# Drains and woven statistics in the GAT passes of a graph network, and a weight product moved between its two GCN passes

## What is computed

```python
h = relu(layernorm(x));  x = x + gat(elu(gat(h, W1)), W2)   # two GAT layers, 4 heads, self loops
h = relu(layernorm(x));  x = x + attention(h)               # 8 heads, exp(clip(q.k)), sum / (z + 1e-9)
h = relu(layernorm(x));  x = x + hyperbolic(h)
h = relu(layernorm(x))
def gcn(x, W, b): return relu(segment_sum((x @ W)[src] * norm, dst) + b)
x = x + (gcn(gcn(h, W6, b6), W7, b7) @ Wp + bp)
```

## Time and profile before

| | us |
|---|---|
| three runs | 6064.08, 6054.41, 6054.90 |
| median | 6054.9 |
| the profiled execution | 6061.28 |
| its span | 6059.5 |
| mean granted TensorE clock, share of full | 0.903 |

### The profile page before, as it was taken

The page is one execution under the profiler, slowest core; times in us unless marked ns, Lnnn a source line. Parts: engine busy times, 40 slices in busy tenths (PEclk is TensorE's granted clock), DMA queues, the critical chain, the costliest instruction groups (busy, mean ns, idle before and its releaser), DMA issues. The chain is left out here.

```text
span 6059.5 us, 76838 instructions
## 1 busy us (share of the span) xinstructions
PE 4625.8 (76%) x20970; PEld 3391.5 (56%) x20970; DVE 4623.4 (76%) x13469; ACT 3032.3 (50%) x7622; POOL 3524.5 (58%) x3009
## 2 busy tenths in 40 slices
PE   4888888888884888856777688888857658996665
PEld 3666666666662666634665455555534435664554
DVE  5888888888886888838999467777768878884555
ACT  2777777777771444423444345555535544441111
POOL 3555454444525777728888277777634425446777
PEclk9999999999996999977888889999977879998877
DMA  3666666666663444425777534544437764444444
GB/s 119 236 243 240 244 241 245 238 242 243 242 232 116 126 127 127 128 72 192 252 240 250 174 117 152 153 154 154 147 111 242 248 220 129 147 138 126 144 152 137
DMA packets 651890, 1096.80 MB, mean 181 GB/s; under 512 B 88662, under 2 KB 472086, under 8 KB 651341
## 3 DMA queue, kind: packets, MB, share of 16 engines
q1 hardware_dynamic: 526026, 837.10, 40.4%
q0 software_dynamic: 125440, 254.79, 14.3%
HBM read 523.88 MB, written 575.95 MB: 182 GB/s over the span
## 5 line engine op out<-in xcount | busy, mean ns | idle before, releaser
L839 PE MATMUL mm<-w,tt 128*128 128x264 f32 x3136 | 737.3, 389 | 0.8 <-ACT tt L883 0.8
L1321 POOL DMA_INDIRECT aim<-F,index x392 | 592.9, 1512 | 119.5 <-issue 119.5
L839 PEld LDWEIGHTS mm<-w,tt 128*128 128x128 f32 x3136 | 585.7, 192 | 92.6 <-ACT tt L883 1.0
L777 POOL DMA_INDIRECT xd<-in_x_dram,index x196 | 219.5, 1120 | 681.3 <-DMA XD<-xd 650.4
L1321 POOL DMA_INDIRECT got<-F,index x392 | 495.5, 1264 | 167.7 <-issue 108.5
L1477 ACT ACTIVATE rows<-acc 128x260 f32<-128x260 f32 (+1 forms) x588 | 227.3, 387 | 646.4 <-PE acc L1468 646.3
L805 POOL DMA_INDIRECT place<-PLACE,place_ix x392 | 425.4, 1085 | 119.5 <-issue 119.5
L1464 PE MATMUL acc<-got,sel 128*128 128x260 f32 (+1 forms) x1176 | 432.7, 455 | 78.9 <-DVE sel L1440 72.5
L829 PE MATMUL tp<-ident,h 128*128 128x128 f32 x1568 | 236.8, 284 | 325.2 <-ACT h L894 163.3
L2476 DVE SCALAR_TENSOR_TENSOR agg<-mask,agg,acc 128x128 f32<-128x128 f32 x784 | 237.5, 345 | 248.5 <-issue 143.8
L839 PE MATMUL mm<-wl,tt 128*128 128x264 f32 x1568 | 421.7, 391 | 5.7 <-ACT tt L883 5.4
(11 more groups left out here) (349 smaller groups left out, 13762.5 us busy)
## 6 DMA issues: line engine op xcount, KB each, us to landing
F<-f1o SPq DMA_DIRECT2D x97, 528.0 KB
F<-f2o SPq DMA_DIRECT2D x97, 528.0 KB, 3.3
HL<-ho SPq DMA_DIRECT2D x97, 528.0 KB, 3.7
xin<-in_x_dram SPq DMA_DIRECT2D x97, 512.0 KB
H<-h SPq DMA_DIRECT2D x97, 512.0 KB, 3.6
X<-x3o SPq DMA_DIRECT2D x97, 512.0 KB, 2.6
out_dram<-oo SPq DMA_DIRECT2D x97, 512.0 KB
drow<-DSTF SPq DMA_DIRECT2D x84, 448.0 KB
```

What stands on the lines that cost most here:

```text
L777: nc.gpsimd.indirect_dma_start(out=xd[:, n % 2, t, :], out_offset=None, in_=x, in_offset=bass.IndirectOffsetOnAxis(ap=index[:, tile, 1:2], ...
L839: last = nc.tensor.matmul(mm[PAIR[stage, q]][:, r, 0:F2W], lhs[:, q, 2 * r + k, :], w[:, k, :], start=(k == 0), stop=(k == KB - 1))
L1321: nc.gpsimd.indirect_dma_start(out=buf[:, n % SLOTS, t, :], out_offset=None, in_=table, in_offset=bass.IndirectOffsetOnAxis(ap=index[:, n ...
```

## The change

1. SoftPass gets `make_way(dve)`: it issues two steps of a generator that the stage may have set (`self.steps`), then a drain of DVE if the stage has `yields` set. GAT1 and GAT2 set it, the hyperbolic pass does not. It stands after the backward scan, after each piece of the message, after `sel`, after the pieces of the own part in `gat_output` (GAT2), and after the first piece of its sum and of its quotient; in GAT1 also after each piece of the ELU and of the own part. That is 10 drains a group in GAT1 and 8 in GAT2.
2. In GAT2 the statistics of group n - 3 (before: n - 2) are issued two steps at each `make_way`, with the rest after the differences. What follows them moves one group: the stores of H2 (n - 4) and Q2 (n - 6), ACT's normalization (n - 4), the product with Wq (n - 5). The loops of DVE, PE, ACT and SP get one iteration more.
3. In the attention pass POOL issues the four degree gathers before `got[1]`.
4. In the first GCN pass the product with W7 is gone. PE multiplies `agg` by W6 into rows of edges, with b6 added by a matmul of ones with three bf16 parts (`b6_parts`); ACT takes the relu to `put`, so T7 holds relu(agg W6 + b6). The statistics are woven into `carry_on`, two steps after each of its eight operations; `carry_on` works for group n - 3 (before n - 2), `select` for n - 1 (before n).
5. In the second GCN pass PE multiplies `agg` by W7 (four matmuls of 128x512 a group) and ACT takes relu and b7 from that.
6. Setup: the constant rows of T7 are relu(b6) with no product; `b6_parts` is made; the load of b6 as a column is gone.

The core of the diff:

```diff
+            def make_way(self, dve):
+
+                take(self.steps, 2)
+                if self.yields:
+                    dve.drain()
...
                 V.tensor_tensor_scan(self.bwd[:, s, ::-1], self.pen[:, s, 1:SE + 1][:, ::-1], self.fwd[:, ::-1], -BIG,
                                      ALU.add, ALU.max).then_inc(self.done["most"], 1)
+                self.make_way(dve)
...
                     V.tensor_tensor(by_head(g[:, k, 0:D], H), by_head(g[:, k, 0:D], H),
                                     per_head(self.w_edge(n)[:, k, :], D // H), ALU.mult)
+                    self.make_way(dve)
...
-                        last = V.tensor_tensor(by_head(o[:, k, :], H), by_head(own[:, k, :], H),
-                                               per_head(self.w_own(n)[:, k, :], D // H), ALU.mult)
-                    link(last)
+                        last = link.go(V.tensor_tensor(by_head(o[:, k, :], H), by_head(own[:, k, :], H),
+                                                       per_head(self.w_own(n)[:, k, :], D // H), ALU.mult))
+                        self.make_way(dve)
+                    link.need(last)
                 for k in PIECES:
                     last = V.tensor_tensor(o[:, k, :], o[:, k, :], rows[:, k, 0:D], ALU.add)
+                    if k is PIECES[0]:
+                        self.make_way(dve)
...
                             ph.select(dve, b).then_inc(d["msg"], 1)
+                            ph.make_way(dve)
                         if within(c):
                             hold(dve, d["exp"], c + 1, None)
                             for k in PIECES:
                                 last = V.scalar_tensor_tensor(o[:, c % SLOTS, k, :], zm[:, k, :], -1.0,
                                                               o[:, c % SLOTS, k, :], ALU.add, ALU.max)
+                                if k is PIECES[0]:
+                                    ph.make_way(dve)
                             last.then_inc(d["g"], 1)
+                            ph.make_way(dve)
...
+                    def shifts(s):
+                        yield from layernorm_stats(nc, link, st, mean[:, :], dm[:, :], var[:, :])
+                        yield from rsqrt(nc, link, rt[:, s, :], var[:, :], ra[:, :], ROOT)
+                        V.scalar_tensor_tensor(nm[:, s, :], mean[:, :], -0.5, rt[:, s, :],
+                                               ALU.mult, ALU.mult).then_inc(d["stats"], 1)
...
-                        a, b, x = n, n - 1, n - 2
+                        a, b, x, y = n, n - 1, n - 2, n - 3
+                        if within(y):
+                            ph.steps = shifts(y % 2)
...
-                        a, b, c, e = n, n - 1, n - 3, n - 4
+                        a, b, c, e = n, n - 1, n - 4, n - 5
...
                         ph.gather(pool, at, 0, bound, d["tp"], at.n * G - G)
-                        ph.gather(pool, at, 1, bound, d["score"], at.n - 1)
                         for t in range(at.n * G, (at.n + 1) * G):
...
+                        ph.gather(pool, at, 1, bound, d["score"], at.n - 1)
...
-            def carry_on(self, dve, at, t):
+            def carry_on(self, dve, at, t, steps=iter(()), each=0):
...
-                last.then_inc(self.done["agg"], 1)
+                    if k == KB - 1:
+                        last.then_inc(self.done["agg"], 1)
+                    take(steps, each)
...
                             for t in range(G):
-                                ph.carry_on(dve, b, t)
-                        if at.alive(NG):
-                            ph.select(dve, at)
-                    pipeline(dve, NG, 2, group)
+                                ph.carry_on(dve, b, t, steps, 2)
+                        take(steps)
+                        if s.alive(NG):
+                            ph.select(dve, s)
+                    pipeline(dve, NG, 3, group)
...
+                                nc.tensor.matmul(bank, ph.agg[:, c.slot, 0, t * P:(t + 1) * P], w6[:, 0, :],
+                                                 start=True, stop=False)
+                                nc.tensor.matmul(bank, ones3[:, :], b6_parts[:, :], start=False, stop=False)
+                                last = nc.tensor.matmul(bank, ph.agg[:, c.slot, 1, t * P:(t + 1) * P], w6[:, 1, :],
+                                                        start=False, stop=True)
...
+                                last = nc.tensor.matmul(m7[o][:, :], w7[:, k, o * P:(o + 1) * P],
+                                                        ph.agg[:, c.slot, k, :], start=(k == 0), stop=(k == KB - 1))
...
+                                nc.scalar.activation(yt[:, c.slot, o, :], m7[o][:, :], ACT.Relu,
+                                                     bias=b7_col[:, o:o + 1]).then_inc(d["yt"], 1)
```

More of the change, by code:

```diff
@@ L503, in _ @@
                     last.then_inc(s_pe, 1)
[L504 to L514, removed]
+                    pe.wait_ge(s_v, 6)
+                    for j in range(KB):
+                        last = nc.tensor.transpose(ps_t[:, j * P:(j + 1) * P], relu_b[:, j * P:(j + 1) * P], ident[:, :])
+                    last.then_inc(s_pe, 1)
+                    pe.wait_ge(s_v, 7)
+                    for j in range(KB):
+                        last = nc.tensor.matmul(ps_t[:, 256:512], relu_bt[:, j, :], wp[:, j, :],
+                                                start=(j == 0), stop=(j == KB - 1))
+                    last.then_inc(s_pe, 1)
                     nc.tensor.matmul(ps_c[:, 0:T], last_row[:, :], dst_col[:, :], start=True, stop=True)\
                         .then_inc(s_pe, 1)
-                    pe.wait_ge(s_v, 10)
+                    pe.wait_ge(s_v, 8)
                     for b in range(NB):
@@ L1238, in __init__ @@
                 self.kinds, self.h, self.width, self.src, self.dst, self.out = kinds, heads, width, src, dst, out
+                self.yields, self.steps = False, iter(())
             def __enter__(self):
@@ L1855, in group @@
                             ph.differences(dve, a)
+                        take(ph.steps)
                         if within(x):
@@ L1890, in group @@
                                 product(qm[:, :], gt[:, m % 2, :, :], wq).then_inc(d["qm"], 1)
-                    every(4, group)
+                    every(5, group)
                 @block.scalar
@@ L2533, in _, with shifts @@
                     dve.wait_ge(d["start"], 1)
+                    def shifts(sl):
+                        yield from layernorm_stats(nc, link, st, mean[:, :], dm[:, :], var[:, :])
+                        yield from rsqrt(nc, link, rt[:, sl, :], var[:, :], ra[:, :], ROOT)
+                        V.scalar_tensor_tensor(nm[:, sl, :], mean[:, :], -0.5, rt[:, sl, :],
+                                               ALU.mult, ALU.mult).then_inc(d["stats"], 1)
                     def group(at):
                         link.restart()
-                        b = at.back(2)
+                        s, b = at.back(1), at.back(3)
+                        steps = iter(())
                         if at.alive(NG):
-                            sl = at.slot
                             ph.gathered(dve, at, pv)
@@ L2625, in gnn_program @@
             yt = ph.sb("yt", [P, 2, KB, G * P])
+            m7 = [ph.ps(f"m7{k}", [P, G * P]) for k in range(KB)]
             mm = [ph.ps(f"mm{k}", [P, 2, D]) for k in range(2)]
```

131 lines of the change are left out of this document (57 added, 74 removed).

## The result

The kernel before took 6055.0 us (median of four runs beside it, 6054.4 to 6064.1), the changed one 5998.8 (5975.0 to 6008.5). The ratio is 0.9898, 95% interval [0.9864, 0.9932]: faster by 56 us, where 23 were forecast. The time lies inside the range and on the side given 0.59. The profiled execution was the fastest of the four, 5975.0 us, with a span of 5973.2; 24 us of its gain are not in the median; the attention pass of that execution is the reason, as the experiments show.

The account below looks back on a forecast made before the run. No engine bounds the whole: POOL nearly full in GAT2, DVE bounding first GCN, POOL second GCN. Terms 6 - 5 + 17 + 0 - 46 + 5 + 0 = -23 from 6061.3, less 6.4, gave 6032 us; range 5974 to 6073.

Parts of the forecast that it names:

- POOL is kept out by DVE's large operations: GAT passes: a gather begun in the backward scan takes 4.38 us; after the change 2.3 us or less.
- The price of a drain, 0.2 us: DVE in GAT1 and GAT2: each drain costs 0.2 us, between 0.08 and 0.33.
- GAT1 +6: GAT1: four drains on the pace-setting loop cost 0.8 us in 8 groups, +6 us, range -15 to +20.
- GAT2 "floor 24.0, -5": GAT2: DVE-PE-ACT floor of 23.0 us plus two drains with statistics gives 24.0 against 24.2 an iteration, -5 us.
- GAT2's tail +17: End of GAT2: statistics one group later leave one uncovered group of 16.65 us, +17 us, range +8 to +22.
- Attention 0: Attention pass: degree gathers moved before got[1] have a group as cover, 0 us, range -5 to +5.
- First GCN -46: First GCN pass: woven statistics save 1.0 us in each of 46 inner groups, -46 us, bounds -55 and -23.
- Second GCN +5: Second GCN pass: W7's matmuls fit PE's idle time and POOL stays the bound, +5 us, range 0 to +15.
- Setup 0: Setup: the removed product chain, 4.23 us, and twelve new operations, 3.5 us, balance to 0.
- B: Rival, chance 0.24: relieved gathers shorten GAT1 and GAT2, GAT2 reaching its 23.0 us floor; kernel 5980 us.
- C: Rival, chance 0.15: later sel lowers PE's granted clock in GAT2 to 0.78, +41 us there; kernel 6073 us.
- D: Rival, chance 0.17: weaving gives half, first GCN -23 us, second GCN +15 us; kernel 6065 us.

Follow-up runs that it names:

- the runs of parts: One part of the change alone against the kernel before: POOL's attention order, ratio 1.0002; GCN passes and setup, 0.9897; GAT1 and GAT2 drains with woven statistics, 1.0009.
- the parts alone: Only the drains in GAT1 and GAT2 and GAT2's woven statistics, against the kernel before: 6065.4 us, ratio 1.0009.
- the part alone: Only the two GCN passes and the setup changed, against the kernel before: 5995.5 us, ratio 0.9897.

## Why the prediction was right, and where its steps were not

The side and the range hold; the size does not: -23 was forecast and -56 measured. The largest miss is the first GCN pass, whose term was put 21 us too small; GAT1's 6 us that did not come and small differences elsewhere are the rest. Point by point, on the profiled run and the runs of parts.

- **"POOL is kept out by DVE's large operations"**: held. The gather fell by 1.7 us (4.38 to 2.69), forecast 2.1, so the sign "2.3 us or less" was missed: it began earlier in the scan, and it ended 0.82 after it, near the 0.87 that I had put as an estimate. The Trainium skill's inference ("SBUF — State Buffer", section "Who interferes with whom"), that tensor_tensor does not stall descriptor generation, is again not borne out: with tensor_tensor pieces directly behind the scan the gather takes 4.4 us, with a drain between them 2.7.
- **The price of a drain, 0.2 us**: 0.15 behind a piece, 0.27 behind a scan; within the bounds of 0.08 and 0.33, though the piece starts 0.07 after its forerunner where I gave 0.1 to 0.25. The Trainium skill, "VectorE: DVE Perf Modes", section "The DRAIN you can't avoid", has the next operation start only when the pipe is empty, by which an explicit drain would be free; the rows differ by the 0.15. The same section adds that an operation which is not held starts earlier, and with that the 0.08 of overlap agrees.
- **GAT1 +6**: 0 (+1 with the parts alone). I had the price of four drains on the loop in the groups where PE is late for the scan. The median group is 26.3 us with drains, without and with twice as many; price and relief both go into DVE's waits.
- **GAT2 "floor 24.0, -5"**: the period is 23.9, -10 over the stage. The floor that I named, DVE, PE and ACT in turn, is what binds: `crow` starts as ACT's exponents end. What I added to it was wrong: the 1.0 us for two pairs with drains between crow and sel (priced at 0.5 each, measured 0.45). Without drains, with sel some 0.3 us earlier, the period is 23.9 all the same; from sel to the exponents it then takes 20.7 us in place of 20.3, and why is open. I also took DVE's work as covered ("DVE works 619 of 775 us"). Eight pairs with drains take about 3.6 us where the row took 3.0, and the cover is down to 0.1 us: twice the drains, and DVE binds.
- **GAT2's tail +17**: +20 (108.6 against 88.6 us). The method, one group with nothing beside it, held.
- **Attention 0**: right on the first chip (1.0002), wrong on the second, where the order is worth 131 us between the medians, and on the third probably, by the size of the gain. The first chip's -33 in the profiled run was luck. The step that failed on the second is "the moved gather has a group as cover". I looked at POOL's busy share (673 of 1020) and did not do the sum that I had done for GAT2: 669 us of work, 176 us of gaps (588 x 0.30) and 85 us of waits for the score are 930 of 1020. So POOL's queue had little room, and something that lengthened the loop could show. That this slack is what hid it on the first chip is my reading, not shown.
- **First GCN -46**: -67, beyond the bound of -55. This is the term of the sum that was mis-sized. I had 1.4 us a group for the weaving and gave back 0.4 for waits that a step might still meet; nothing was to be given back: a pair costs 0.205 us in place of some 0.35, the group lost 1.3 (9.08 to 7.79 in the mean, -62 over 48 groups), to the 7.7 that the slot loop was put at (7.8). The bound was too tight by its own numbers, for 1.4 us over 46 groups is 64 and the slot loop allowed 60. The ends, which the sum left out, add the rest: about +5 at the start, where the first carried sum comes a group later, and -10 at the end, where W7's steps are missing.
- **Second GCN +5**: +9 in the profiled run, +7 with the part alone. PE is busy 468 us in place of 343 and its granted clock is 0.91 in place of 0.79, so its cover held with less room than the 236 idle us suggest.
- **Setup 0**: 75 us before and after.
- **Rivals.** B (relief reaches the end) came about in no run: GAT2's floor of 23.0 was not reached, the period is 23.8 to 23.9 with drains, without, and with one. C (half clock in GAT2): not seen, 0.82 before and after; its sum is also 5 us short, since +41 in place of -5 gives 6078 and not 6073. D: the reverse happened. E: excluded by 2.69 us.

What stays open: why the old order's attention pass takes 1020 us on one chip and 1181 on another. A later landing of the gathers goes with it; whether it is the cause was not tried. Open too is what starts the better way of running the attention pass, which one of the profiled runs with the new order had on the first chip and two had not.

## What to carry to other kernels

For an engine that only issues transfers, add up work, the gap after each issue, and waits, before calling a place in its queue slack; a wait in the middle of its order holds everything behind it. Weave short dependent steps behind independent work, but leave nothing behind the pair that empties the pipe; place a drain only where one long operation is followed by others and a transfer is held, and look first whether it is held there: behind the scan of GAT2, with short dependent steps woven in, it was not. A wait that disappears is a gain only if nothing else waits in its place: look for what releases the next step before calling an engine the bound. Before a stage's length is explained from one profile, look whether its groups all run alike: two periods that alternate with the granted clock can be worth more than the change itself.

## What the runs showed that I had not expected

- A pass whose groups alternate between 18.2 and 19.8 us on an unchanged instruction stream, in number as many as the stretches at the half level of the clock (1.2 in place of 2.4 GHz), with one wait of PE of 2.19 us a group for ACT. One run left this for 25 groups, in most of which the wait was in two pieces of about 0.7 and 1.3 us. Filling the wait with products took 50 us out of a stage of 1037.
- The kernel before differs by 3.8% between chips (6056 to 6284 us), the changed one by 1.5% (5999 to 6092).
- A drain behind a drain costs 0.05 us; a drain behind a piece 0.15; one behind a scan over 4 partitions 0.27.
- With two short dependent steps behind the scan and no drain, the held gather ends 0.81 us after the scan in place of 2.96, as it does with a drain.
